# Cross-attention in a decoder kernel: scores turned by transposes, with the maximum subtracted on GpSimd

## The chip, the cores and the metric

The kernel runs on one core of a Trainium2 chip. The metric is the device time of one execution in microseconds; the lower the better.

## The reference

The program is a decoder of two layers over 8 sequences of 256 tokens of width 128: sliding-window attention with a memory that learns, a cross-attention, routed experts, causal attention, a gated recurrence, and a feed-forward mixture, each followed by a residual and a normalisation. The change lies in the cross-attention of the first layer and in the part of the memory's MLP that is computed in the same loop:

```python
# cross-attention: 16 heads of 8, query and context of 256 tokens
scores = einsum('bhqd,bhkd->bhqk', q, k) / sqrt(8)
scores = where(mask, scores, -1e9)
attn = softmax(scores, axis=-1)
x = einsum('bhqk,bhkd->bhqd', attn, v)
# memory MLP of the layer before it (updated weights)
out_mem = silu(x_in @ w1.T + b1) @ w2.T + b2
out_merged = sigmoid(out_swa @ lin1.T) * out_swa + sigmoid(out_mem @ lin2.T) * out_mem
```

The product of query and key is kept near f32 precision by splitting each into three bf16 parts; six pairs of parts are stacked along the contraction axis (6 x 16 = 96 rows).

## The kernel before, in words

Each engine has its own instruction stream, written by hand: PE (products and transposes), DVE, ACT, GpSimd (pool) and SyncE (sp), which issues the loads. They meet only through semaphores: an instruction adds to one (`then_inc`), and another engine waits for a count (`wait_ge`). The order inside an engine is the order of the code. PSUM has eight banks of 128 x 512 f32.

The cross-attention runs in four steps of NB = 2 batches (T = 512 tokens). Each engine has a function `mix(i, following)` for step i; three steps run in a loop (Fori) and the last stands behind it. A step has XU = 32 units, one for each pair of batch and head. Beside its own units, step i computes the *head* of step i+1: `keys` (the key projection) and parts 0 to 9 of `head`. Parts 0 to 3 are the four hidden chunks of the MLP (a product z, then Silu with the bias b1), part 4 the lin1 gate, part 5 the product with w2, part 6 the lin2 gate, parts 7 and 8 merge, normalise and transpose, and part 9 gives the query projection, which DVE splits into q_parts. The parts share bank 1. Tables (`early`, `later`) say behind which unit each part stands on each engine. The head of step 0 runs ahead of the loop, one part after another.

One unit, before:

- PE, `scores_q(n)` (L1074): two products give the scores with the queries on the partitions, 128 x 256 each, in one bank (`q_bank`). AHEAD = 14 units of them run ahead of the rest.
- DVE (L1815): a fused add of the mask and maximum over the keys, two per unit, written back to the bank; the maximum goes to `mx`. After every eight units PE transposes the maxima (`maxima_T`, L1084) and DVE negates them and splits them into three bf16 parts, `neg_max` (`negated`, L1804 to L1808).
- PE, `scores_k(n)` (L1102, L1104, L1105): the scores again, now with the keys on the partitions, plus the mask and the negated maximum as two further accumulating products; six products of 256 columns per unit. sT_ready.
- ACT (L1509): one exponential of 128 x 512 from the bank to `pT`.
- PE, `values(b, g)` (L1115): after four heads, eight products with `v_aug` (values and a column of ones, for the sum). ACT copies the result (`copy_outputs`, L1498), PE transposes it (`outputs_T`, L1127), DVE divides by the sum (L1831, L1834).

Behind a step's units comes the tail, the same in both kernels: output projection, residual, normalisation, router, ranks and slots of the experts (DVE, up to L1891). Then GpSimd scatters the tokens to the experts' rows with eight indirect DMAs (L817).

GpSimd otherwise splits the keys of the next step (`split_k`, L795 to L797), and makes add_q and add_k from the masks (L803, L804). SyncE saves the split parts to DRAM (`save_k`, `save_q`) and loads them back stacked (`stack`: 12 loads to `k_stack`, L658, and six to `q_stack`, L662). In a step the stack loads wait for sT_ready of all 32 units, since both kinds of scores read the stacks; the next step's first scores wait for them (L1064, L1065).

## Time and profile before

| | us |
|---|---|
| median of 3 runs | 1086.91 |
| lowest, highest | 1083.47, 1094.82 |
| the profiled execution, its device time | 1093.54 |
| its span, first to last instruction | 1091.5 |
| busy in the span: PE, DVE, ACT, GpSimd | 767.9, 529.8, 393.6, 158.9 |
| the four steps of this stage, from the first scores | from 342.6 to about 620 |
| mean granted clock of TensorE | 0.832 |

Durations below come from that one profiled execution. Its busy times are sums of an engine's instructions; matmuls are pipelined, so the spacing of their starts tells more than the length of one. The granted clock is given as a share of full speed: 1.0 is 2.4 GHz, 0.5 is 1.2 GHz. The releaser of a wait is inferred from the semaphores; "issue" is time in which an engine waited for nothing that the profile shows.

### The profile page before, as it was taken

To read this page: it belongs to the slowest core of one execution; us is meant where nothing else is said; L and a number is where in the kernel's file an instruction comes from. 1 tells how busy PE (TensorE), PEld (TensorE's weight loads), DVE (VectorE), ACT (ScalarE), POOL (GpSimd) and SP (SyncE) were. 2 spreads that over 40 slices of the span, in tenths; PEclk is the share of its full clock that TensorE was granted. 3 is DMA by queue.
4 is the path that set the end of the run, shared out by engine and by line. 5 is a ranking of instruction groups with operands and counts; after the bars stand their busy time and mean duration, and the time that the engine had idled before them with its cause. 6 is when DMAs were issued, how large, how long until landed. Compare 5 with 4: busy or idle time off the path is not lost.

```text
span 1091.5 us, 14695 instructions
## 1 busy us (share of the span) xinstructions
PE 767.9 (70%) x4586; PEld 496.2 (45%) x4586; DVE 529.8 (49%) x1947; ACT 393.6 (36%) x924; POOL 158.9 (15%) x207
## 2 busy tenths in 40 slices
PE   5888787968453986977968919992664664664664
PEld 4445353544121663653645617882442442442442
DVE  4244253443333945936939321112556556556556
ACT  3514434252111542533532513330343343343343
POOL 9200000000101004013012040002040040040020
PEclk8798998999566997997977959997887887887886
DMA  7400000000106035054040011311000010010000
GB/s 220 144 7 13 1 19 0 19 0 0 53 22 103 2 54 93 0 64 81 9 64 20 2 43 37 91 49 44 20 25 6 29 24 5 29 24 5 10 0 10
DMA packets 49236, 39.37 MB, mean 36 GB/s; under 512 B 11234, under 2 KB 42658, under 8 KB 49188
## 3 DMA queue, kind: packets, MB, share of 16 engines
q1 hardware_dynamic: 47140, 34.62, 14.7%
q0 software_dynamic: 2048, 4.20, 1.4%
q8 instruction: 19, 0.31, 0.1%
q14 instruction: 29, 0.24, 0.1%
HBM read 27.20 MB, written 11.60 MB: 36 GB/s over the span
## 4 chain that ended last, share of the span: by engine, by line
PE 52%; DVE 20%; issue 11%; ACT 8%; DMA 5%; POOL 2%; SPq 2%; DVEq 0%; POOLq 0%; ACTq 0%
PE bank L1219 4%; DMA q_stack<-parts_dram 4%; PE bank L1208 4%; DVE R L2066 2%; PE bank L1102 2%; PE bank L960 2%; PE bank L1105 2%; PE bank L1104 2%; PE bank L1115 2%; PE bank L892 2%; PE bank L1022 2%; PE bank L1074 2%; PE bank L1029 2%; PE bank L1298 2%; PE bank L983 2%
## 5 line engine op out<-in xcount | busy, mean ns | idle before, releaser
L1815 DVE CUSTOM_DVE_ANT_0 bank<-bank,add_q 128x256 f32<-128x256 f32 x256 | 100.2, 458 | 45.2 <-PE bank L1074 29.6
L1509 ACT ACTIVATE pT<-bank 128x512 f32<-128x512 f32 x128 | 76.1, 597 | 73.7 <-PE bank L1105 71.4
L1074 PE MATMUL bank<-k_stack,q_stack 96*128 96x256 bf16 x256 | 52.1, 303 | 40.0 <-DMA q_stack<-parts_dram 34.8
L1238 PE MATMUL bank<-ident,X 128*128 128x128 f32 x48 | 14.3, 420 | 89.7 <-DVE X L1923 89.7
L1102 PE MATMUL bank<-q_stack,k_stack 96*128 96x256 bf16 x256 | 70.4, 275 | 2.1 <-DVE mx L1815 2.1
L1104 PE MATMUL bank<-add_k,ident_b 128*128 128x256 bf16 x256 | 70.8, 276 | 0.0
L1105 PE MATMUL bank<-neg_max,head_sel 96*128 96x256 bf16 x256 | 70.7, 276 | 0.0
L1298 PE MATMUL bank<-XT,kpad 128*128 128x256 f32 (+1 forms) x256 | 59.1, 364 | 3.3 <-DVE cT L2023 3.2
L2023 DVE TENSOR_TENSOR cT<-bank,decay 128x384 f32<-128x384 f32 x64 | 35.7, 558 | 43.8 <-POOL decay L847 43.3
L1298 PEld LDWEIGHTS bank<-XT,kpad 128*128 128x128 f32 x256 | 47.9, 210 | 16.5 <-DVE cT L2023 9.5
L1074 PEld LDWEIGHTS bank<-k_stack,q_stack 96*128 96x128 bf16 x256 | 25.3, 105 | 64.8 <-DMA q_stack<-parts_dram 31.8
L1534 ACT ACTIVATE he<-bank 128x324 f32<-128x324 f32 x64 | 28.2, 441 | 69.4 <-PE bank L1208 63.9
L1238 PEld LDWEIGHTS bank<-ident,X 128*128 128x128 f32 x48 | 8.0, 167 | 98.7 <-DVE X L1923 95.5
L847 POOL TENSOR_SCALAR_AFFINE_SELECT decay<-decay 128x256 f32<-128x256 f32 x64 | 26.1, 408 | 142.8 <-ACT decay L1587 142.8
L795 POOL TENSOR_TENSOR qr<-g,k_parts 128x512 f32<-128x512 f32 x4 | 4.6, 1161 | 282.8 <-ACT k_parts L1480 282.7
L837 POOL DMA_INDIRECT pair_rows<-expert_out,spot_i x32 | 30.6, 956 | 102.9 <-DMA expert_out<-rows_y 93.2
L1219 PEld LDWEIGHTS bank<-moe_w,he 128*108 128x108 f32 x384 | 42.8, 173 | 1.3
L1219 PE MATMUL bank<-moe_w,he 128*108 128x128 f32 x384 | 43.1, 273 | 0.0
L1586 ACT ACTIVATE decay<-bank,a_col 128x256 f32<-128x256 f32 x64 | 30.6, 478 | 32.4 <-PE bank L1317 31.8
L1908 DVE COPY rows_y<-bank 108x384 f32<-108x384 f32 x16 | 8.9, 558 | 67.1 <-PE bank L1219 67.1
L1208 PE MATMUL bank<-rowsT,moe_w 128*128 128x324 f32 x128 | 39.1, 461 | 3.3 <-DVE rowsT L1900 3.3
L1404 ACT ACTIVATE probs<-probs,stats 128x192 f32<-128x192 f32 (+1 forms) x68 | 29.6, 436 | 20.5 <-DVE stats L1652 20.5
(401 smaller groups left out, 1775.0 us busy)
## 6 DMA issues: line engine op xcount, KB each, us to landing
k_stack<-parts_dram SPq DMA_DIRECT2D x48, 64.0 KB
q_stack<-parts_dram SPq DMA_DIRECT2D x24, 128.0 KB, 10.1
expert_in<-no_rows SPq DMA_DIRECT2D x8, 324.0 KB, 3.9
rows<-expert_in SPq DMA_DIRECT2D x8, 324.0 KB
expert_out<-rows_y SPq DMA_DIRECT2D x8, 324.0 KB
moe_w<-in_L_ffn_w_dram SPq DMA_DIRECT2D x1, 2048.0 KB
parts_dram<-k_parts SPq DMA_DIRECT2D x4, 384.0 KB, 2.7
parts_dram<-q_parts SPq DMA_DIRECT2D x12, 128.0 KB, 1.7
```

The source lines that it names most:

```text
L837: pool.indirect_dma_start(pair_rows[:, n, :], None, expert_out, bass.IndirectOffsetOnAxis(spot_i[:, n:n + 1], 0)).then_inc(gathered.sem, 16)
L1074: last = pe.matmul(q_bank(n)[:, c * S:(c + 1) * S], q_stack[:, h // 2, b * S + c * P:b * S + (c + 1) * P], k_stack[:, h // 2, h % 2, b * S ...
L1102: pe.matmul(dst, k_stack[:, h // 2, h % 2, b * S + c * P:b * S + (c + 1) * P], q_stack[:, h // 2, b * S:(b + 1) * S], start=True, stop=False)
L1104: pe.matmul(dst, ident_b[:], add_k[:, b * QC + c, :], start=False, stop=False)
L1105: last = pe.matmul(dst, head_sel[:, h % 8, :], neg_max[:, (n // 8) % 2, :], start=False, stop=True)
L1208: pe.matmul(bank[4 + n % 4][:, 0:HALF], moe_w1[:, e, k * P:(k + 1) * P], rowsT[:, e % 2, half * HALF:(half + 1) * HALF], start=True, stop= ...
L1219: last = pe.matmul(bank[2 + part][0:ROWS, t * P:(t + 1) * P], he[:, e % 2, k, col:col + ROWS], moe_w2[:, e, k, :], start=(k == 0), stop=(k ...
L1298: pe.matmul(m_banks(n)[1][:, lo:lo + width], kpad2[:, h, b * S + c * P:b * S + (c + 1) * P], XT[:, q0:q0 + width], start=True, stop=True)
L1509: act.activation(pT[:, g % 2, j], k_bank(n)[:].rearrange("p (c q) -> p c q", c=QC), ACT.Exp).then_inc(exp_ready.sem, 1)
L1586: act.activation(decay[:, n % DEEP, 0:S], eb[:, 0:S], ACT.Exp, bias=a_col[:, b * QC, h:h + 1])
L1815: last = dve.tensor_tensor_reduce(sc, sc, add_q[:, b * QC + c, :], 1.0, 2.0 * NEG, ALU.add, ALU.max, mx[:, c, h:h + 1])
L2023: dve.tensor_tensor(cT[:, g, j, :], m_banks(n)[1][:, 0:S + P], decay[:, n % DEEP, :], ALU.mult).then_inc(c_ready.sem, 1)
```

## The change

The second set of scores goes. DVE's fused add and maximum now writes the masked scores to SBUF, into one of SLIDE = 4 buffers `shifted`. GpSimd subtracts the row's maximum (stretched over 256 keys) in place for three units of four; for the fourth (`on_act`, n % 4 == 3) it only negates the maximum, and ACT takes the exponential in place with it as bias (two instructions of 128 x 256). PE then transposes the unit in four 128 x 128 blocks (`scores_T`) into one of two banks, and ACT's exponential takes it to `pT` (a plain copy in the fourth unit). The scores run LEAD = 3 units ahead instead of 14, since only three banks hold them, and DVE's unit n waits for the transposes of unit n - 4.

```diff
+                def scores_T(n):
+
+                    if on_act(n):
+                        pe.wait_ge(*p_ready.at(i, n // 4 + 1))
+                    else:
+                        pe.wait_ge(*s_shifted.at(i, n + 1))
+                    if n >= 2:
+                        pe.wait_ge(*exp_ready.at(i, n - 1))
                     for c in range(QC):
-                        dst = k_bank(n)[:, c * S:(c + 1) * S]
-                        pe.matmul(dst, k_stack[:, h // 2, h % 2, b * S + c * P:b * S + (c + 1) * P],
-                                  q_stack[:, h // 2, b * S:(b + 1) * S], start=True, stop=False)
-                        pe.matmul(dst, ident_b[:], add_k[:, b * QC + c, :], start=False, stop=False)
-                        last = pe.matmul(dst, head_sel[:, h % 8, :], neg_max[:, (n // 8) % 2, :], start=False, stop=True)
+                        for k in range(QC):
+                            last = pe.transpose(sT_bank(n)[:, k * S + c * P:k * S + (c + 1) * P], shifted[:, n % SLIDE, c, k * P:(k + 1) * P], ident[:])
                     last.then_inc(sT_ready.sem, 1)
...
+                for n in range(LEAD):
+                    scores(n)
+                for n in range(XU):
+                    if n + LEAD < XU:
+                        scores(n + LEAD)
+                    scores_T(n)
+                    if n >= 5 and n % 4 == 1:
+                        values((n // 4 - 1) // G, (n // 4 - 1) % G)
...
+                    if following and n == 1:
+                        keys(i + 1)
+                    if following and n in pe_at:
+                        head(i + 1, pe_at[n])
```

DVE and ACT, a unit:

```diff
                     wait_apart(dve, passed, *s_ready.at(i, n + 1))
+                    if n >= SLIDE:
+                        wait_apart(dve, passed, *sT_ready.at(i, n - SLIDE + 1))
                     for c in range(QC):
-                        sc = q_bank(n)[:, c * S:(c + 1) * S]
-                        last = dve.tensor_tensor_reduce(sc, sc, add_q[:, b * QC + c, :], 1.0,
-                                                        2.0 * NEG, ALU.add, ALU.max, mx[:, c, h:h + 1])
+                        last = dve.tensor_tensor_reduce(shifted[:, n % SLIDE, c, :], q_bank(n)[:, c * S:(c + 1) * S], add_q[:, b * QC + c, :], 1.0,
+                                                        2.0 * NEG, ALU.add, ALU.max, mx[:, n % SLIDE, c:c + 1])
                     last.then_inc(s_read.sem, 1)
...
+                    if on_act(n + 1):
+                        act.wait_ge(*s_shifted.at(i, n + 2))
+                        for c in range(QC):
+                            rows = shifted[:, (n + 1) % SLIDE, c, :]
+                            last = act.activation(rows, rows, ACT.Exp, bias=neg_mx[:, c:c + 1])
+                        last.then_inc(p_ready.sem, 1)
                     act.wait_ge(*sT_ready.at(i, n + 1))
...
-                    act.activation(pT[:, g % 2, j], k_bank(n)[:].rearrange("p (c q) -> p c q", c=QC), ACT.Exp).then_inc(exp_ready.sem, 1)
+                    act.activation(pT[:, g % 2, j], sT_bank(n)[:].rearrange("p (c q) -> p c q", c=QC), ACT.Copy if on_act(n) else ACT.Exp).then_inc(exp_ready.sem, 1)
```

GpSimd gets the units, and with them the scatters of the step before (one behind every third unit) and split_k (behind unit 4); add_k and its mask load go:

```diff
+            def heads(i, following):
+                for n in range(XU):
+                    wait_apart(pool, passed, *s_read.at(i, n + 1))
+                    if on_act(n):
+                        pool.tensor_scalar(neg_mx[:], mx[:, n % SLIDE], -1.0, None, ALU.mult).then_inc(s_shifted.sem, 1)
+                    else:
+                        pool.tensor_tensor(shifted[:, n % SLIDE], shifted[:, n % SLIDE], mx[:, n % SLIDE].unsqueeze(2).to_broadcast([P, QC, S]), ALU.subtract).then_inc(s_shifted.sem, 1)
+                    if following and n == 4:
+                        split_k(i + 1)
+                    if not is_first(i) and n % 3 == 2 and n // 3 < PAIRS:
+                        scatter(i - 1, n // 3)
                 if following:
+                    masks(i + 1)
```

Silu in the head's parts 0 to 3 becomes z (1 + tanh(z/2)), with the half taken at the w2 result: ACT computes the tanh and a copy of z with its bias, DVE the product. PE's next product into bank 1 waits for ACT's copy.

```diff
-                    act.activation(hT[:, n, 0:T], bank[1][:], ACT.Silu, bias=b1_new[:, n:n + 1]).then_inc(hT_b.sem, 1)
...
+                    act.activation(hT[:, n, 0:T], bank[1][:], ACT.Tanh, bias=b1_half[:, n:n + 1], scale=0.5)
+                    act.activation(z_of[n % 2], bank[1][:], ACT.Identity, bias=b1_new[:, n:n + 1]).then_inc(z_act.sem, 1)
...
+                    dve.scalar_tensor_tensor(hT[:, n, 0:T], hT[:, n, 0:T], 1.0, z_of[n % 2], ALU.add, ALU.mult).then_inc(hT_b.sem, 1)
```

The parts stand behind other units: on PE 0 to 9 behind units 3, 5, 7, 9, 11, 13, 15, 18, 23, 25, on ACT behind nearly the same, on DVE behind 7 to 28. The output transposes and divisions are done per half of the queries, those of batch 0 inside the step.

SyncE: the stack loads are split, and in a step they wait for the scores alone:

```diff
             save_k(0)
+            stack_k(0)
             save_q(0)
-            stack(0)
+            stack_q(0)
...
-                    sp.wait_ge(*sT_ready.at(i))
-                    stack(i + 1)
+                    sp.wait_ge(*s_ready.at(i))
+                    stack_k(i + 1)
+                    stack_q(i + 1)
```

How the streams now stand. PE, a unit deep in a step, before (the names are the stacked keys and queries, the mask, and the negated maxima):

```order
L1074 MATMUL bank4<-k_stack,q_stack 128x256 [waits s_read]
L1074 MATMUL bank4<-k_stack,q_stack 128x256
L1102 MATMUL bank6<-q_stack,k_stack 128x256 [waits exp_ready]
L1104 MATMUL bank6<-add_k,ident_b 128x256
L1105 MATMUL bank6<-neg_max,head_sel 128x256
```

The last three rows stand twice per unit, once for each half of the keys. PE after the change, unit 3 with the head's part 0 behind it and the next unit (k_copied is the semaphore under p_ready):

```order
L1103 MATMUL bank<-k_stack,q_stack 128x256 [waits s_read]
L1103 MATMUL bank<-k_stack,q_stack 128x256
L1111 ISA
L1118 MATMUL bank<-ident,shifted 128x128 [waits exp_ready,k_copied]
L1118 MATMUL bank<-ident,shifted 128x128 x3
L1050 ISA
L1051 REGISTER_ALU [waits b_x_loaded]
L1054 MATMUL bank<-xT_in,w1T_new 128x512 [waits kf_ready]
```

The unit's transposes now wait for ACT (in the other three of four for GpSimd's s_shifted), and the head's product stands right behind them. GpSimd in the loop, before:

```order
L795 TENSOR_TENSOR qr<-g,k_parts 128x512 [waits kh_ready]
L84 ISA
L796 CAST k_parts<-qr 128x512 [waits pool_b]
L101 REGISTER_ALU
L797 TENSOR_TENSOR k_parts<-qr,k_parts 128x512 [waits pool_b]
L84 ISA
L84 ISA [waits sT_ready]
L803 TENSOR_SCALAR add_q<-mask_q 128x1024 [waits masks_loaded]
L804 TENSOR_SCALAR add_k<-mask_k 128x1024
```

GpSimd in the loop after the change, units 2 to 5 (max_a is the semaphore under slots_ready, L831 the subtraction, L829 the negation):

```order
L831 TENSOR_TENSOR shifted<-shifted,mx 128x512 [waits s_read]
L84 REGISTER_ALU
L823 DMA expert_in<-Xm,slot_i 6208x128 [waits max_a]
L84 REGISTER_ALU
L829 TENSOR_SCALAR neg_mx<-mx 128x2 [waits s_read]
L84 REGISTER_ALU
L831 TENSOR_TENSOR shifted<-shifted,mx 128x512 [waits s_read]
L807 REGISTER_ALU
L809 TENSOR_TENSOR qr<-g,k_parts 128x512 [waits kh_ready]
L84 ISA
L810 CAST k_parts<-qr 128x512 [waits pool_b]
```

The scatters, which stood in one block behind the tail, and split_k now stand between the units' subtractions.

## Rows read from the trace of the kernel before

**Rows 1.** windows: a step's scores, then what lies between two steps; busy us (x instructions)

```profile
342.60:398.30 55.70, 52.28 (x413) 33.97 (x416) 41.16 (x174) 30.37 (x49) 3.16 (x4) 0.97 0.07 22
398.30:419.00 20.70, 8.69 (x79) 6.70 (x72) 9.17 (x55) 3.04 (x10) 5.62 (x6) 0.72 1.00 110
419.00:475.60 56.60, 53.57 (x416) 33.95 (x420) 40.60 (x174) 30.40 (x49) 9.79 (x11) 0.95 0.09 30
```

**Rows 2.** page, part 5; busy us, mean ns of one, idle before and its releaser

```profile
L1815 DVE CUSTOM_DVE_ANT_0 bank<-bank,add_q 128x256 f32<-128x256 f32 x256 | 100.2, 458 | 45.2 <-PE bank L1074 29.6
L1509 ACT ACTIVATE pT<-bank 128x512 f32<-128x512 f32 x128 | 76.1, 597 | 73.7 <-PE bank L1105 71.4
```

**Rows 3.** timeline of PE in step 0; start us, us

```profile
350.45 1.13 PE L1022 MATMUL bank<-xT_in,w1T_new 128*128 128x512 f32 x2 [0.34 <-ACT hT L1458]
...
356.22 3.70 PE L1029 MATMUL bank<-hT,w2T_new 128*128 128x512 f32 x8 [0.30 <-ACT g L1462]
...
360.86 0.27 PE L1102 MATMUL bank<-q_stack,k_stack 96*128 96x256 bf16 x1
360.97 0.27 PE L1104 MATMUL bank<-add_k,ident_b 128*128 128x256 bf16 x1
...
371.20 0.60 PE L1037 MATMUL bank<-ident,g 128*128 128x128 f32 x4
...
379.73 1.07 PE L1115 MATMUL bank<-pT,v_aug 128*32 128x256 f32 x16
```

**Rows 4.** timeline around the steps' ends; engine (SPq: SyncE's queue), line, idle before

```profile
324.80 4.18 SPq L658 DMA_DIRECT2D k_stack<-parts_dram  x12
...
342.64 0.60 PE L1074 MATMUL bank<-k_stack,q_stack 96*128 96x256 bf16 x2 [19.97 <-DMA q_stack<-parts_dram]
...
395.74 2.59 ACT L1509 ACTIVATE pT<-bank 128x512 f32<-128x512 f32 x4
...
397.81 4.12 SPq L658 DMA_DIRECT2D k_stack<-parts_dram  x12
...
416.88 0.17 DVE L1891 TENSOR_TENSOR gates_all<-share,found 128x8 f32 x1
...
418.97 0.61 PE L1074 MATMUL bank<-k_stack,q_stack 96*128 96x256 bf16 x2 [5.15 <-DMA q_stack<-parts_dram]
...
424.44 0.43 DVE L1815 CUSTOM_DVE_ANT_0 bank<-bank,add_q 128x256 f32<-128x256 f32 x1 [7.39 <-issue]
...
572.73 0.43 DVE L1815 CUSTOM_DVE_ANT_0 bank<-bank,add_q 128x256 f32<-128x256 f32 x1 [0.85 <-PE bank L1074]
...
617.74 2.59 ACT L1509 ACTIVATE pT<-bank 128x512 f32<-128x512 f32 x4 [0.15 <-PE bank L1105]
```

**Rows 5.** groups of GpSimd, shapes kept apart; columns as in rows 2

```profile
L817 POOL DMA_INDIRECT expert_in<-Xm,slot_i x32 | 31.4, 980 | 34.2 <-DVE slot_i L1886 25.7 <-issue 8.5
...
L843 POOL TENSOR_SCALAR v_aug<-ctx_tok 128x512 f32<-128x512 f32 x4 | 6.0, 1498 | 90.8 <-DVE X L1923 90.8
L789 POOL TENSOR_TENSOR x_res<-memT,x_bo_rows 128x512 f32<-128x512 f32 x4 | 5.1, 1264 | 23.5 <-DVE memT L1772 23.5
L795 POOL TENSOR_TENSOR qr<-g,k_parts 128x512 f32<-128x512 f32 x4 | 4.6, 1161 | 282.8 <-ACT k_parts L1480 282.7
```

**Rows 6.** timeline of GpSimd

```profile
346.57 1.15 POOL L795 TENSOR_TENSOR qr<-g,k_parts 128x512 f32<-128x512 f32 x1 [27.27 <-ACT k_parts L1480]
...
418.71 0.98 POOL L817 DMA_INDIRECT expert_in<-Xm,slot_i  x1 [0.30 <-issue]
...
655.12 0.15 POOL L831 MEMSET v_aug<- 128x32 f32 x1
```

**Rows 7.** timeline of ACT in step 0

```profile
346.51 1.28 ACT L1458 ACT_TABLE_LOAD   x1
347.81 0.69 ACT L1458 ACTIVATE hT<-bank,b_new 128x512 f32<-128x512 f32 x1
```

**Rows 8.** window early in the last step; PE, PEld, DVE, ACT, POOL, PEclk, DMA, GB/s

```profile
574.00:584.00 10.00, 6.17 (x25) 2.31 (x24) 9.86 (x48) 0.00 (x0) 6.03 (x7) 0.50 0.12 46
```

More of the change, by code:

```diff
@@ L822, in _ @@
             pool.wait_ge(*slots_zero.at(0))
-            with pool.Fori(0, STEPS - 1) as i:
-                mix(i, True)
-            mix(STEPS - 1, False)
+            heads(0, True)
+            with pool.Fori(0, STEPS - 2) as i:
+                tail(i, True)
+                heads(i + 1, True)
+            tail(STEPS - 2, True)
+            heads(STEPS - 1, False)
+            tail(STEPS - 1, False)
+            for n in range(PAIRS):
+                scatter(STEPS - 1, n)
             pool.wait_ge(*scattered.at(STEPS - 1))
@@ L1057, in values_of @@
                 last.then_inc(v_b.sem, 1)
-            early = {0: "keys", 2: 0, 4: 1, 6: 2, 8: 3, 10: 4, 12: 5}
-            later = {4: 6, 9: 7, 17: 8, 20: 9}
             def mix(i, following):
@@ L1110, in values @@
                     pe.wait_ge(*exp_ready.at(i, b * H1 + 4 * g + 4))
+                    if b == 0 and g == 0:
+                        pe.wait_ge(*slots_ready.before(i))
                     if g % 2 == 0 and (b > 0 or g > 0):
@@ L1125, in outputs_T @@
                     for g in range(G):
-                        for c in range(QC):
-                            last = pe.transpose(bank[2 + c][:, g * P:(g + 1) * P], o_heads[:, g, c * P:(c + 1) * P], ident[:])
+                        last = pe.transpose(o_bank(b, c)[:, g * P:(g + 1) * P], o_heads[:, g, c * P:(c + 1) * P], ident[:])
                     last.then_inc(o_tr.sem, 1)
-                for n in range(AHEAD):
-                    scores_q(n)
-                    if n == 9:
-                        maxima_T(0)
-                    if following and n in early:
-                        if n == 0:
-                            keys(i + 1)
-                        else:
-                            head(i + 1, early[n])
@@ L1837, in mix @@
+                    if following and n in dve_at:
+                        head(i + 1, dve_at[n], head_chain)
+                for c in range(QC):
+                    outputs_of(1, c)
                 if following:
@@ L2074, in _ @@
             head_chain = Chain(dve, dve_h, 0)
-            for n in range(4, 10):
+            for n in range(10):
                 head(0, n, head_chain)
```

193 lines of the change are left out of this document (80 added, 113 removed).

## The prediction, made before the changed kernel had run

> **What bounds the kernel now.** I read the cores' spans first (one core, 1091.5 us), then the windows. The change touches the cross-attention stage: a prologue, four steps of 32 head units, and a serial tail behind each step. In the windows [rows 1] a step's scores run 55.7 us in step 0 and 56.6 us in step 1; PE is busy 52.3 and 53.6 us of them, at a granted clock of 0.97 and 0.95 of 2.4 GHz. DVE has 41, ACT 30, GpSimd 3 to 10 us. So PE bounds this stretch. The groups of the page say the same: ACT's exponential idled 73.7 us, nearly all until PE's L1105, and DVE's masked maximum until PE's L1074 [rows 2]. The timeline gives PE's price by start to start at full clock: a 256-column bf16 product every 0.11 us [rows 3], so a unit costs PE 2 + 6 of them, 0.88 us.
>
> Between two steps lie 20.7 us [rows 1] in which PE works 8.7 us, the clock falls and the 16 DMA engines are busy throughout. The timeline [rows 4] shows why: the last exponential of step 0 ends at 398.3, the stack loads go out from 397.81 (they wait for sT_ready of all units), PE's next scores start at 418.97, released by the q_stack load, and DVE's first maximum only at 424.44, after 7.39 us marked issue, which is neither data nor a semaphore; DVE's tail had ended at 417.05. Behind step 2 there is no such gap (the loop is left there): DVE starts at 572.73.
>
> **The change, part by part.** PE: six products per unit (0.66 us) become four 128x128 f32 transposes. Four took 0.60 us [rows 3] with about 0.27 of pipeline end in it, so 0.11 each and 0.44 a unit. Over 32 units that is 7 us off; the eight small transposes of the maxima go too. What is left on PE in a step: units 32 x 0.66 = 21.1; eight value products at 1.0 = 8.0; the first half's output transposes 0.9; of the next step's head seven products at 0.97 = 6.8, w2 3.5, two sets of transposes 0.9, q 0.9 [rows 3]. Sum 42.1 us, against 52.3 busy before.
>
> DVE: the same two reductions per unit, 100.2 us / 128 = 0.78 us a unit [rows 2], now written to SBUF instead of PSUM; I take the same price (bounds: 0.1 us less or more). The negated maxima go, four products come, priced at 0.69 us each, which is what ACT's Silu of that shape takes [rows 7]. DVE stays near 37 us.
>
> GpSimd is new in the chain. The trace has no 128x512 subtraction with a stretched operand in two rows of 256; the bounds are 1.16 us (two plain operands) and 1.50 us (one operand, 16-column pieces), and nearest is 1.26 us, a two-operand add with a repeated operand [rows 5]. I take 1.27 with its start. The negated maximum of the fourth unit has 256 numbers: 0.15 us for a tiny memset [rows 6] up to 0.35; I take 0.25. A step then costs 24 x 1.27 + 8 x 0.25 = 32.5 us, plus split_k's three instructions 3.1, plus, from step 1 on, eight scatters of the step before at 0.98 + 0.30 = 1.28 [rows 5, 6] = 10.2. Sum: 35.6 in step 0, 45.8 in steps 1 and 2, 42.7 in step 3. GpSimd, idle so far, becomes the longest engine in three steps of four.
>
> Whether it slows beside DVE: with the maxima running, L795 took 1.15 us against a group mean of 1.16 [rows 6, 5]; no cost. The Trainium skill's SBUF page ("Who interferes with whom") says that a VectorE instruction with two SBUF inputs shuts out a GpSimd instruction that reads SBUF. The maximum has one of its inputs in PSUM, so by the rule it stays free and the trace agrees. By the same rule the new products of the head, both operands in SBUF, would each hold back one subtraction by up to 0.7 us, some 3 us a step. I leave that out of the sum.
>
> ACT: 32 exponentials or copies at 0.60 = 19.2 [rows 2]; 16 exponentials of half the size, at most 0.5 each = 8; four output copies 2.4; keys 1.3; four times Tanh and Identity at 0.69 = 5.5; 2.3 for the rest; a table load fewer (1.28 [rows 7]; Tanh and Exp share a set, Silu did not), two left = 2.6. Some 41 us. In units 3 to 10 it needs 3.0 us for two units, so it paces those, at 1.5 to 1.7 us a unit; GpSimd's scatters (1.4 us a unit there) lie beside it.
>
> Time of a step. Step 0: PE's 42.1, the pipe to fill before the first transposes (0.8 + 1.3) and to drain (0.6), and 3 us since PE starts at 1.2 GHz: 48 against 55.7, so -7.7. Steps 1 and 2, from DVE's start: GpSimd's 45.8, fill and drain 2.2, and 3 us for stalls around the 3.5 us w2 block, over which only three units lie ready: 51, against 475.6 - 424.44 = 51.2 in step 1 (step 2 is alike): 0 each. Step 3: 42.7 + 2.2 + 2 cold = 47 against 620.3 - 572.7 = 47.6: -0.6.
>
> Between steps. SyncE now waits for s_ready of all units, which PE reaches at n=28, about 3 units before the end; q's saves hang on DVE's head part 9, at the same place. So the loads start some 3 us earlier, and so does all that is behind them in the DMA queues. PE's scores could start 3 us earlier; DVE's start after the 7.39 us gap I take 3 us earlier too, since the gap ends just after the DMA traffic does (bounds 0 and 5). Behind step 2 DVE's own tail ends 0.85 us before it starts; at most 0.5 is won. Together -6.5. The scatters no longer stand between the tail and split_k; nothing waits for either there.
>
> Prologue. The head of step 0 runs one part after another, PE waiting for ACT to free the bank; Identity adds 4 x 0.69 = +2.8 us. But the 12 key loads no longer wait behind q: from the first stack load, 324.80, to the scores, 342.64, were 17.8 us [rows 4], and the six q loads are half the bytes: 8.9 us. With the saves before them I take -8 (bounds 0 and -10). Net -5.
>
> Sum: -5 - 7.7 - 0 - 0 - 0.6 - 6.5 = -19.8 us. The profiled execution took 1093.54 us, so 1073.7 for it. It lies 6.6 above the median of the three runs, 1086.91, and from that the sum gives 1067.
>
> **The rivals.**
> A, GpSimd's subtraction is dearer and nothing is won. At the upper bound of 1.50 us (L843 [rows 5]) 96 of them cost 96 x 0.23 = 22 us more, in three steps fully on the path, with held-back starts by DVE in it: 1067 + 22 = 1089. For it: GpSimd's rows for one shape differ by 0.35 us, and each instruction now has a wait. Against: L843's odd pieces.
>
> B, slower: PE stays at 1.2 GHz. Early in step 3 PE was busy 62% for ten microseconds and the clock stayed at 0.5 [rows 8]; only a solid block of products raised it. The Trainium skill's TensorE page ("PE-mode transpose") says the full clock does not engage for transposes. With the clock at half a unit costs PE 0.44 + 0.88 + 0.5 for its share of the values = 1.8 us. In step 3, which has no head, all 32 units would run so: 58 + 3 = 61 instead of 47, +14. In the others the clock would rise with w2 (unit 13); until then 13 x 1.32, six products at 2.1 and two value blocks at 2 make 34 us instead of 21: +13, three times. 1067 + 53 = 1120. It decides once PE is slower than GpSimd, at 1.27 us a unit. Against: each step's head products start early, and before they raised the clock within 4 to 6 us; step 3 has value blocks every fourth unit. Nothing in the trace is a long run of transposes, so it can't be excluded.
>
> C, the engines overlap without the stalls that I added and the loads land earlier: steps of 45, 48, 48, 45 and 2 us more in each gap: 1067 - 11 - 6 = 1050, or less if a subtraction costs 1.16 (-8): 1042.
>
> **How the numbers follow.** Forecast 0.50 (own range 1053 to 1078), A 0.23, B 0.13, C 0.14. The range 1040 to 1104 takes in C and A and leaves out B's far end. A measurement of this kernel can tell about 1% (11 us) from no change. Faster by more: C and nine tenths of the forecast, 0.59. Slower: B and a few hundredths of A beyond its bound, 0.16. Within 1%: the rest, 0.25.
>
> **What would show it.** Right: GpSimd near 46 us busy in steps 1 and 2 and the longest engine, its subtraction at 1.2 to 1.3 us start to start, transposes 0.11 us apart with the clock near 1, first scores of step 0 near 335, DVE's first maximum of step 1 some 23 us after the last exponential. Wrong: transposes 0.21 us apart deep in a step (B); subtractions at 1.5 us or waits of PE on s_shifted in all units (A); steps over 55 us with no engine full, which would mean that the ring DVE, GpSimd, PE, ACT with four buffers is bound by its handovers, and none of my sums.

## The result, and the profile after

The changed kernel is slightly slower: 1093.26 us median (1086.06 to 1098.77, 20 runs) against 1088.76 (1081.56 to 1094.82, 20 runs), ratio 1.004 with a 95% interval of 1.0021 to 1.0059. The forecast was 1067. The profiled execution's span is 1097.0 us against 1091.5; these two executions took 1098.77 and 1093.54 us, both some 5 above their kernel's median, and the steps below are read from them.

The page's busy times and costliest groups after (columns as in [rows 2]):

```profile
PE 753.1 (69%) x4298; PEld 485.6 (44%) x4298; DVE 517.8 (47%) x1884; ACT 422.0 (38%) x1001; POOL 268.6 (24%) x330
...
L1834 DVE CUSTOM_DVE_ANT_0 shifted<-bank,add_q 128x256 f32<-128x256 f32 x256 | 95.2, 420 | 76.7 <-PE bank L1103 67.8
L831 POOL TENSOR_TENSOR shifted<-shifted,mx 128x512 f32<-128x512 f32 x96 | 100.4, 1060 | 91.2 <-DVE mx L1834 75.0
L1525 ACT ACTIVATE pT<-bank 128x512 f32<-128x512 f32 x128 | 75.4, 596 | 95.9 <-PE bank L1118 94.5
L1118 PE MATMUL bank<-ident,shifted 128*128 128x128 f32 x512 | 86.7, 297 | 34.3 <-POOL shifted L831 20.7
```

PE is busy 15 us less, GpSimd 110 us more, and the time is no better. The last columns tell how that can be: DVE waits for PE's scores, GpSimd for DVE's maxima, PE for GpSimd, ACT for PE. Each engine waits for the one ahead of it, and the four form a ring; before, DVE and ACT waited mostly for PE [rows 2]. GpSimd's subtraction, feared at up to 1.50 us, takes 1.06.

The windows after, cut as [rows 1], with step 3 as a fourth: step 0, the gap, step 1, step 3.

```profile
329.69:390.42 60.73, 49.80 (x344) 30.99 (x344) 36.68 (x158) 37.09 (x68) 32.33 (x36) 0.90 0.13 32
390.42:406.39 15.97, 8.31 (x71) 6.53 (x71) 7.36 (x43) 3.01 (x9) 2.26 (x2) 0.78 1.06 106
406.39:474.20 67.81, 51.20 (x344) 31.59 (x344) 40.72 (x172) 37.19 (x68) 41.00 (x44) 0.85 0.12 31
577.74:622.49 44.75, 35.88 (x318) 24.59 (x314) 27.43 (x150) 26.60 (x51) 34.34 (x40) 0.89 0.04 13
```

In step 1 no engine is full: PE 51 of 67.8 us, GpSimd and DVE 41. PE is still the busiest, and its busy time has hardly fallen: 51.2 us against 53.6 in step 1, 49.8 against 52.3 in step 0 [rows 1]. Below, a step is measured from DVE's first maximum to the last exponential, and a gap from there to DVE's next first maximum:

| us | step 0 | step 1 | step 2 | step 3 | three gaps |
|---|---|---|---|---|---|
| before | 54.9 | 51.1 | 51.0 | 47.6 | 26.1, 26.6, 19.6 |
| after | 59.9 | 62.3 | 61.1 | 41.2 | 21.5, 24.6, 21.5 |
| after less before | +5.0 | +11.2 | +10.1 | -6.4 | -4.6, -2.0, +1.9 |

So +19.9 in the steps and -4.7 in the gaps. The prologue, from its first load (xT_in, 279.93 before, 275.57 after) to the first scores, went from 62.7 to 54.1 us, -8.6. The stage itself began 4.4 us earlier, ahead of all changed code; in the executions profiled here that start lies between 269.5 and 283.7, so profiled executions are compared by step and not by total. What lies behind the last exponential is 3.4 us longer, in unchanged code. The five add up to the difference of the spans, +5.6 us.

How far two executions of the same code differ is seen where an edit left the steps alone. The run with the old order of the loads (below) has the steps of the changed kernel and took 59.9, 60.0, 61.5 and 41.3 us; the same reading of the two versions of the kernel before (below) gives a gap that differs by 3.4 us. So a difference under some 2 us in one step, or 3.5 us in one gap, shows nothing by itself. Step 1 in the changed kernel and in that run:

```profile
411.95:474.20 62.25, 49.74 (x338) 30.86 (x338) 38.72 (x158) 37.19 (x68) 41.00 (x44) 0.88 0.11 29
420.06:480.08 60.02, 47.16 (x338) 29.48 (x338) 38.98 (x158) 37.04 (x68) 40.99 (x44) 0.94 0.11 28
```

The longer one has the lower granted clock. In it the clock was at 1.2 GHz not only at the start but once more in the middle of the step, behind waits of 0.37 and 1.40 us of PE for GpSimd, and PE worked through this stretch:

```profile
454.13:457.53 3.40, 3.40 (x25) 1.69 (x24) 1.40 (x8) 2.84 (x6) 2.61 (x4) 0.50 0.06 22
```

The place where a step with a head loses is seen in three stretches of step 1. PE at its start, and in the MLP's region (start us, us):

```profile
406.39 1.46 PE L1103 MATMUL bank<-k_stack,q_stack 96*128 96x256 bf16 x6 [0.76 <-DMA q_stack<-parts_dram]
412.79 0.61 PE L1103 MATMUL bank<-k_stack,q_stack 96*128 96x256 bf16 x2 [4.94 <-DVE mx L1834]
414.01 1.11 PE L1118 MATMUL bank<-ident,shifted 128*128 128x128 f32 x4 [0.61 <-POOL shifted L831]
...
416.19 1.91 PE L1084 MATMUL bank<-ctxT,w_L_xattn_wkT 128*128 128x512 f32 x2
...
428.65 0.65 PE L1118 MATMUL bank<-ident,shifted 128*128 128x128 f32 x4 [1.27 <-ACT shifted L1520]
429.14 1.02 PE L1054 MATMUL bank<-xT_in,w1T_new 128*128 128x512 f32 x2
430.00 0.38 PE L1103 MATMUL bank<-k_stack,q_stack 96*128 96x256 bf16 x2
430.23 0.60 PE L1118 MATMUL bank<-ident,shifted 128*128 128x128 f32 x4
```

GpSimd, DVE and ACT around the w2 block, which keeps PE busy from 439.7 to 443.3:

```profile
440.26 1.04 POOL L831 TENSOR_TENSOR shifted<-shifted,mx 128x512 f32<-128x512 f32 x1 [0.80 <-DVE mx L1834]
444.92 1.04 POOL L831 TENSOR_TENSOR shifted<-shifted,mx 128x512 f32<-128x512 f32 x1 [3.62 <-DVE mx L1834]
```

```profile
443.96 0.42 DVE L1834 CUSTOM_DVE_ANT_0 shifted<-bank,add_q 128x256 f32<-128x256 f32 x1 [3.88 <-PE bank L1103]
```

And the other way round, DVE in the head's part 9 (two of its five instructions left out) and PE behind it:

```profile
464.75 0.75 DVE L1800 TENSOR_SCALAR g<-bank,x_bq 128x512 f32<-128x512 f32 x1 [0.78 <-PE bank L1079]
...
466.72 0.43 DVE L1804 CAST q_parts<-qr 128x512 bf16<-128x512 f32 x1
467.18 0.69 DVE L1806 TENSOR_TENSOR q_parts<-qr,q_parts 128x512 bf16<-128x512 f32 x1
467.79 0.42 DVE L1834 CUSTOM_DVE_ANT_0 shifted<-bank,add_q 128x256 f32<-128x256 f32 x1
```

```profile
466.15 0.63 PE L1118 MATMUL bank<-ident,shifted 128*128 128x128 f32 x4
469.84 0.66 PE L1118 MATMUL bank<-ident,shifted 128*128 128x128 f32 x4 [3.06 <-POOL shifted L831]
```

A block of 3.5 us on PE stops DVE for 3.88 and GpSimd for 3.62; a block of 3.0 us on DVE stops PE for 3.06. Nothing is in hand on either side. And at the step's start PE stands idle 4.94 us for DVE's first maximum. DVE came as late before (424.44, 5.47 us behind PE's first scores; 411.95, 5.56 us behind, after), and what held it there the profile does not show, but PE then ran the head's keys and part 0 meanwhile:

```profile
419.50 2.08 PE L1051 MATMUL bank<-ctxT,w_L_xattn_wkT 128*128 128x512 f32 x2
...
422.35 2.08 PE L1022 MATMUL bank<-xT_in,w1T_new 128*128 128x512 f32 x2
```

### The profile page after: what moved, and what is told of

The parts are those of the page before. It is cut to its first block, busy times and chain, and to the rows that moved or that the text cites. A ratio compares the mean times of both kernels' runs of the same rounds, so it can differ in the third digit from the quotient of the medians.

```text
span 1097.0 us, 14728 instructions
## 1 busy us (share of the span) xinstructions
PE 753.1 (69%) x4298; PEld 485.6 (44%) x4298; DVE 517.8 (47%) x1884; ACT 422.0 (38%) x1001; POOL 268.6 (24%) x330
## 4 chain that ended last, share of the span: by engine, by line
PE 49%; DVE 21%; issue 13%; ACT 9%; POOL 5%; DMA 2%; DVEq 1%; SPq 0%; POOLq 0%; ACTq 0%
PE bank L1229 4%; PE bank L1218 4%; PE bank L1118 3%; PE bank L1130 3%; DVE R L2073 2%; PE bank L992 2%; PE bank L924 2%; PE bank L1308 2%; POOL shifted L831 2%; PE bank L1015 2%; DVE shifted L1834 2%; PE bank L980 2%; PE bank L1062 1%; PE bank L1017 1%; PE bank L1054 1%
## 5 line engine op out<-in xcount | busy, mean ns | idle before, releaser
L1834 DVE CUSTOM_DVE_ANT_0 shifted<-bank,add_q 128x256 f32<-128x256 f32 x256 | 95.2, 420 | 76.7 <-PE bank L1103 67.8
L831 POOL TENSOR_TENSOR shifted<-shifted,mx 128x512 f32<-128x512 f32 x96 | 100.4, 1060 | 91.2 <-DVE mx L1834 75.0
L1118 PE MATMUL bank<-ident,shifted 128*128 128x128 f32 x512 | 86.7, 297 | 34.3 <-POOL shifted L831 20.7
L1118 PEld LDWEIGHTS bank<-ident,shifted 128*128 128x128 f32 x512 | 63.5, 151 | 51.5 <-POOL shifted L831 28.8
L1103 PE MATMUL bank<-k_stack,q_stack 96*128 96x256 bf16 x256 | 54.1, 303 | 24.7 <-DVE mx L1834 13.7
L1308 PE MATMUL bank<-XT,kpad 128*128 128x256 f32 (+1 forms) x256 | 62.2, 378 | 3.2 <-DVE cT L2030 3.2
L1308 PEld LDWEIGHTS bank<-XT,kpad 128*128 128x128 f32 x256 | 50.2, 219 | 17.2 <-DVE cT L2030 8.8
L1103 PEld LDWEIGHTS bank<-k_stack,q_stack 96*128 96x128 bf16 x256 | 26.1, 107 | 50.0 <-DVE mx L1834 19.0
L1503 ACT ACTIVATE log_var<-mv,eps 128x2 f32<-128x2 f32 x34 | 9.8, 289 | 80.3 <-DVE mv L1770 80.0
```

The costliest lines, as they stand in the source:

```text
L831: pool.tensor_tensor(shifted[:, n % SLIDE], shifted[:, n % SLIDE], mx[:, n % SLIDE].unsqueeze(2).to_broadcast([P, QC, S]), ALU.subtract).t ...
L1103: last = pe.matmul(q_bank(n)[:, c * S:(c + 1) * S], q_stack[:, h // 2, b * S + c * P:b * S + (c + 1) * P], k_stack[:, h // 2, h % 2, b * S ...
L1118: last = pe.transpose(sT_bank(n)[:, k * S + c * P:k * S + (c + 1) * P], shifted[:, n % SLIDE, c, k * P:(k + 1) * P], ident[:])
L1308: pe.matmul(m_banks(n)[1][:, lo:lo + width], kpad2[:, h, b * S + c * P:b * S + (c + 1) * P], XT[:, q0:q0 + width], start=True, stop=True)
L1834: last = dve.tensor_tensor_reduce(shifted[:, n % SLIDE, c, :], q_bank(n)[:, c * S:(c + 1) * S], add_q[:, b * QC + c, :], 1.0, 2.0 * NEG, A ...
```

## The experiments

Where no range of times is given, a version ran once. Steps and gaps are each from one profiled execution, with the spread told above.

**A deeper ring.** Scores 5 units ahead instead of 3, six buffers `shifted` instead of four, two of `neg_mx`, and DVE's head parts two units later.

```diff
-        LEAD = 3
-        SLIDE = 4
+        LEAD = 5
+        SLIDE = 6
```

> The changed kernel with a deeper pipe: scores run 5 units ahead instead of 3, six buffers of masked scores instead of four, two negated maxima, and DVE's parts of the head two units later. In the changed kernel the steps run 59.9, 62.3, 61.1 and 41.2 us from DVE's first maximum to the last exponential. Theory R (ring: with three units of lead every head part that blocks one engine stops all of them, once its length exceeds what lies ready): the three steps with a head lose 4 to 9 us each, the last at most 1; total -12 to -25 us. Theory G (GpSimd's work, with scatters and port waits, sets the step): no step moves by more than 1 us.

Measured: 1083.62 us median (1081.03 to 1087.95, 10 runs) against 1087.23, ratio 0.9974 (0.9941 to 1.0007). Steps 56.5, 56.2, 56.4, 40.5: 3.4, 6.1 and 4.7 us less than after. The window of step 1 from DVE's first maximum, and who PE waits for in it (us in total, times, longest), the same view of after behind it:

```profile
408.20:464.40 56.20, 45.99 (x338) 28.91 (x338) 44.31 (x158) 36.53 (x68) 39.85 (x44) 0.95 0.09 27
```

```profile
PE bank L1118 <- ACT shifted L1520: 5.8, 5, 1.4
PE bank L1103 <- DVE mx L1834: 4.3, 1, 4.3
PE bank L1118 <- POOL shifted L831: 1.0, 1, 1.0
```

```profile
PE bank L1118 <- POOL shifted L831: 6.5, 5, 3.1
PE bank L1103 <- DVE mx L1834: 4.9, 1, 4.9
PE bank L1118 <- ACT shifted L1520: 3.1, 3, 1.3
```

The waits for GpSimd fall from 6.5 to 1.0 us; those for ACT's in-place exponential grow from 3.1 to 5.8. The version wins back about half of the loss in steps 1 and 2 (6.1 of 11.2 and 4.7 of 10.1 us), and the next handover of the ring takes over. Part of it may be the clock, 0.95 in step 1 against 0.88; the two were not separated. The three gaps are 3.0 us longer in all, and the device time, each version against the kernel before as it ran beside it, falls by 0.7% and not by the 14.8 us of the four steps.

**Part 9 in pieces.** DVE's five instructions for the query parts spread over the last four units.

```diff
-25: 8, 28: 9}
+25: 8, 28: 13, 29: 10, 30: 11, 31: 12}
```

> The changed kernel, but the five DVE instructions of head part 9 (3.0 us in a row behind unit 28) are spread behind units 28 to 31. Theory R: GpSimd's idle time of 3.5 us and PE's of 3.1 us near the end of the steps with a head go, each such step is 2 to 3 us shorter. Theory G: nothing moves. In both the query parts are saved up to 3 us later, so the gap behind the step can grow by that.

Steps 57.2, 58.7, 58.8, 41.2, that is 2.7, 3.6 and 2.3 us less than after, where PE had waited 3.06 us. PE's longest wait for GpSimd in step 1 is 1.4 us now, but its waits there add up to 15.2 us against 15.8, and the clock is 0.95 against 0.88:

```profile
417.45:476.16 58.71, 46.19 (x338) 28.90 (x338) 38.95 (x158) 37.07 (x68) 41.93 (x44) 0.95 0.07 23
```

So removing the block helped, and the higher clock has a part in it that was not separated. The gaps grew by 3.3, 1.8 and -0.4, perhaps since q's parts are saved later, so the total, 1098.5, shows nothing.

**The scatters in one block.** GpSimd's eight scatters again behind the tail, as before the change.

```diff
-                    if not is_first(i) and n % 3 == 2 and n // 3 < PAIRS:
-                        scatter(i - 1, n // 3)
...
+                for n in range(PAIRS):
+                    scatter(i, n)
```

> The changed kernel, but the eight scatters stand in one block behind the tail, as before the change, not between the units. Theory G: steps 1 and 2 lose most of the 8 x 1.2 = 10 us of scatters and come to the length of step 0 or under, 52 to 60 us, and step 3 loses the same, to 32 to 36 us. Theory R: steps 1 and 2 lose 0 to 3 us, step 3 (41.2 us, no head) loses 4 to 10 us since only there GpSimd is the longest engine. The block may delay the start of steps 1 to 3 by some us, as GpSimd's first subtraction stands behind it.

1116.91 us, steps 58.3, 65.1, 66.3, 47.5. GpSimd in front of step 1's first subtraction:

```profile
416.84 1.21 POOL L823 DMA_INDIRECT expert_in<-Xm,slot_i  x1 [6.40 <-DVE slot_i L1891]
...
426.01 0.97 POOL L823 DMA_INDIRECT expert_in<-Xm,slot_i  x1 [0.30 <-issue]
427.00 3.04 POOL L831 TENSOR_TENSOR shifted<-shifted,mx 128x512 f32<-128x512 f32 x3
```

DVE's first maximum was at 420.78, and the first subtraction stands 6.2 us behind it. This is worse, so the scatters between the units are well placed. Counted from GpSimd's first subtraction step 1 took 58.8 us against 61.3: without the scatters between the units it is 2.5 us shorter, not 10, so they are not the main part of what makes the steps long.

**No unit with the bias on ACT.** GpSimd subtracts in all 32 units.

```diff
-            return n % 4 == 3
+            return False
```

> The changed kernel, but GpSimd subtracts in all 32 units and ACT never takes an exponential in place. GpSimd gets 8 x (1.06 - 0.37) = 5.5 us a step more, ACT 8 us less. Theory G: every step 3 to 6 us longer, the last one too. Theory R with ACT's order as the cause (ACT takes the exponential of unit 3, 7, 11 behind a head part, PE waited 1.27 us for it): steps with a head 2 to 5 us shorter, the last step longer by 3 to 6 us.

1100.25 us, steps 58.2, 62.6, 60.4, 44.7. In the steps with a head the eight subtractions more on GpSimd cost nothing that can be told (-1.7, +0.3, -0.7); in step 3, which has none, they cost 3.5. So GpSimd's work sets the pace where there is no head, and does not where there is one.

**ACT's parts one unit later.** They stand behind the next exponential, so that unit 7's and 11's in-place exponentials come ahead of them.

```diff
-        act_at = {3: 0, 5: 1, 7: 2, 9: 3, 11: 4, 15: 6,
+        act_at = {4: 0, 6: 1, 8: 2, 10: 3, 12: 4, 15: 6,
```

> The changed kernel, but ACT takes the head's parts 0 to 4 one unit later (behind units 4, 6, 8, 10, 12), so that it does not stand and wait for PE's product. In the changed kernel two units take 3.65 us in this region, in which PE, ACT and GpSimd all idle. Theory V (convoy: product on PE, then Tanh and Identity, then the exponentials, each in order behind the other; a loop of two engines): the period falls to about 3.0 us and steps 0 to 2 lose 3 to 4 us each, step 3 nothing. Theory G (GpSimd's work sets the step): no change.

1094.93 us, steps 60.1, 61.9, 60.5, 41.2, all within 0.6 of after. PE's waits for L1520 in step 1 fall from 3.1 to 2.2 us, and 3.0 us of new waits for ACT stand ahead of the head's products: what is taken from one wait comes back in another.

**w2 in four pieces.** PE's block of eight products behind units 12 to 15, two at a time; the parts 5 and 6 stand one unit later on ACT and DVE too.

```diff
-                if n == 5:
+                if n == 5 or n >= 50:
...
-        pe_at = {... 11: 4, 13: 5, 15: 6, ...}
+        pe_at = {... 11: 4, 12: 50, 13: 51, 14: 52, 15: 53, 16: 6, ...}
```

> The changed kernel, but the 3.5 us block of w2 products on PE is taken in four pieces behind units 12 to 15, and the parts 5 and 6 stand one unit later. Theory R (a block on one engine stops the ring): the 3.6 us in which DVE and GpSimd idle behind unit 13 go, steps 0 to 2 lose 2 to 3 us each, the last nothing. Theory G: no change.

1092.96 us, steps 60.8, 63.6, 63.8, 41.2: 0.9, 1.3 and 2.7 longer, where 2 to 3 shorter was expected; only the last is clear of the spread. DVE's longest wait for PE in step 1 fell from 3.9 to 2.2 us, so the edit did what it should, while PE's own waits came to 17.9 us for 15.8. While PE runs w2 it works, and the others' idle time then is not lost for PE's sum.

**All together.** The deeper ring, w2 in pieces, ACT's parts later, part 9 behind the last unit, keys behind the first scores.

```diff
+                    if following and n == 2:
+                        keys(i + 1)
...
+        pe_at = {3: 0, 5: 1, 7: 2, 9: 3, 11: 4, 13: 50, 14: 51, 15: 52, 16: 53, 18: 6, 20: 7, 24: 8, 26: 9}
+        act_at = {4: 0, 6: 1, 8: 2, 10: 3, 12: 4, 19: 6, 22: 7, 25: 8}
+        dve_at = {10: 0, 12: 1, 14: 2, 16: 3, 18: 4, 22: 5, 24: 6, 26: 7, 28: 8, 31: 9}
```

> The changed kernel with everything together: 5 units of lead and six buffers, ACT's parts one unit behind PE's, w2 in four pieces, head part 9 on DVE behind the last unit, key projection before the units (in the gap in which PE waits for DVE). If theories R and V name the whole loss, steps 0 to 2 come near the busy time of their longest engine, GpSimd's 42 to 44 us and PE's 42, and take 48 to 52 us instead of 59.9, 62.3 and 61.1; total 1058 to 1070. If the port shared by DVE and GpSimd or GpSimd's work holds them, they stay at 55 to 57 us, as with the deeper pipe alone, total about 1082.

1088.37 us (1085.62 to 1096.79, 10 runs), ratio 0.9994 (0.9957 to 1.0031); steps 56.1, 57.8, 57.1, 40.6. No better than depth alone: the gains of single edits do not add.

**The head out of the steps.** Deeper ring; keys, split_k and all ten parts behind the units.

```diff
-                    if following and n in pe_at:
-                        head(i + 1, pe_at[n])
...
+                    keys(i + 1)
                     values_of(i + 1)
+                    for n in range(10):
+                        head(i + 1, n)
```

> The deeper version (scores 5 units ahead, 6 buffers, 2 of the negated maxima) with keys, split_k and all ten parts of the next step's head taken out from between the units and put behind them, on every engine. It tells how much of a step is units alone. Read from DVE's first maximum to the last exponential, steps 0 to 2 were 56.5, 56.2, 56.4 us in the deeper version and step 3, which has no head, 40.5. Theory H (the units' ring is fast by itself, 40 to 42 us, whatever else PE, DVE and ACT do; the head's parts between the units cost their own 16 us): steps 0 to 2 fall to 40 to 43 us, with the scatters still among them. Theory S (something in the looped steps other than the head holds them, the cold clock at their start, the scatters or the late start of DVE): they stay above 48. The whole kernel gets slower under both, since the head then runs one part after another: the gaps between the steps grow by 20 to 27 us each, device time 1105 to 1125.

1159.87 us. Steps 35.8, 40.7, 40.6, 40.6; gaps 64.3, 67.0, 61.6, so 40 us more each and not 20 to 27. The windows of steps 0 and 1:

```profile
335.33:371.12 35.79, 33.65 (x310) 24.01 (x307) 24.20 (x132) 25.99 (x51) 27.10 (x33) 0.92 0.04 10
435.41:476.10 40.69, 35.25 (x306) 24.55 (x306) 24.61 (x132) 26.50 (x51) 35.36 (x41) 0.90 0.04 14
```

This is the run that divides a step. The units alone take 35.8 us; with the eight scatters, and behind a late start of DVE, 40.7 (+4.9, GpSimd then being the fullest beside PE). The head adds 20.7 us in step 0 and 15.5 in step 1 of the deeper version. PE's work for the head comes to 12.1 us at full clock by the prediction's own prices (6.8 + 3.5 + 0.9 + 0.9): in this ring the head comes on top of the units, with 3 to 9 us more. The windows say how: PE is busy 33.65 of the 35.8 us in the units alone, so there is little room on it. Of the 15.5 us in step 1 of the deeper version 10.7 are more busy time of PE (45.99 against 35.25) and 4.8 more idle time. Before the change a head added 3.5 us in steps 1 and 2 (51.1 less 47.6) and 7.3 in step 0. The 3.5 flatter the kernel before: keys and part 0 stood ahead of DVE's first maximum there, and step 3 ran at a clock of 0.83. Counted from the first scores a head added 7.3 to 8.2 us before and 16 to 23 after the change.

**The head's products left out.** Deeper ring; DVE's four products z (1 + tanh) give way to a tiny instruction, so the MLP's hidden values are wrong.

```diff
-                    dve.scalar_tensor_tensor(hT[:, n, 0:T], hT[:, n, 0:T], 1.0, z_of[n % 2], ALU.add, ALU.mult)
+                    dve.tensor_scalar(hT[:, n, 0:2], hT[:, n, 0:2], 1.0, None, ALU.add)
```

> The deeper version with the head's four products of 128x512 on DVE (z times one plus tanh, both operands in SBUF) left out: DVE adds 1 to two columns instead, so the MLP's hidden values are tanh(z/2) and not silu. Theory L (the product keeps GpSimd's subtraction out and is itself kept waiting by it, 0.7 to 3.5 us instead of 0.69): steps 0 to 2 fall by 2 to 4 us each, from 56.5, 56.2, 56.4 to some 53, device time down by 6 to 12. Theory N (DVE has slack there, the stalls sit elsewhere in the head): under 1 us a step, device time within 3 us.

1086.37 us, steps 56.5, 55.9, 56.7, 40.5: within 0.3 of the deeper version. The products were held up badly (last section), 22.6 us for twelve instead of 8.3, and taking them away gives nothing, though DVE is busy 40.9 us in step 1 instead of 44.3. So DVE's busy time is not the bound either. PE's waits of 1.26 us for ACT's L1520 stand as they did.

**Keys and parts 0 and 1 back in the gap.** Deeper ring; on PE they stand behind the first three scores, on ACT ahead of the units, and DVE's parts 0 and 1 behind units 4 and 6.

```diff
+                    if following and n == 2:
+                        keys(i + 1)
+                        head(i + 1, 0)
+                        head(i + 1, 1)
```

> The deeper version with keys and the head's parts 0 and 1 moved from behind units 1, 3 and 5 to the start of the step, behind the first three scores, as they stood before the change: PE and ACT wait there for DVE's first maximum anyway (PE idled 4.9 us in step 1 of the changed kernel). Theory F (part of the lost time is that the old order filled this gap with the head and the new one does not): each step with a head gets 2 to 4 us shorter from first scores to last exponential, the TensorE clock rises earlier, device time down by 6 to 10 from the deeper version's 1083.6 to some 1075, ratio to before 0.988. Theory N: moving them gains nothing, within 2 us of 1083.6.

1082.71 us (1079.13 to 1087.08, 10 runs), ratio 0.9976 (0.9944 to 1.0007). Steps 60.0, 55.7, 55.1, 40.6, gaps 23.2, 23.7, 18.9. From the first scores to the last exponential step 1 took 61.0 us, as in the deeper version (464.36 - 403.28 = 61.1), and step 0 took 3.5 more: in step 0 there is no idle gap to fill (DVE starts 0.8 us behind the scores), so 6 us of head work delayed the units. Nothing of the 6 to 10 us expected.

**The loads' order alone.** The kernel before, with only the 12 key stack loads of the prologue ahead of q's saves.

```diff
             save_k(0)
+            stack_k(0)
             save_q(0)
-            stack(0)
+            stack_q(0)
```

> The kernel before, with one part of the change alone: in the prologue of the stage the 12 key loads go out before the query parts are saved, not behind them. The prologue (first load of the stage to the first scores, 62.7 us before, 54.1 in the changed kernel, which also has 2.3 us more of Identity) should shorten by 10 to 11 us, the steps stay: total 1077 to 1080. If the loads only ran faster in the changed kernel for another reason (one mask load less), it stays within 2 us.

1075.53 us (1071.98 to 1077.37, 4 runs) against 1089.79, ratio 0.9862 (0.9819 to 0.9904). PE's wait ahead of the first scores is 9.47 us in place of 19.97 [rows 4], and the prologue 52.1 us in place of 62.7:

```profile
327.69 0.61 PE L1078 MATMUL bank<-k_stack,q_stack 96*128 96x256 bf16 x2 [9.47 <-DMA q_stack<-parts_dram]
```

This version is faster than both kernels: one piece of the change, made alone.

**The changed kernel with the old order of those loads.**

```diff
-            stack_k(0)
             save_q(0)
+            stack_k(0)
             stack_q(0)
```

> The changed kernel with only the order of the loads in the prologue put back: the 12 key stack loads go out behind the saves of q's parts again, as before the change. It closes the account of the change. The same edit made alone on the kernel before gave 1075.5 against 1089.8 us, 10.6 of them in the prologue. Theory P (the change holds one gain, the loads' order, and without it the turned scores cost the steps' +20 less the gaps' -5): the prologue from the first load to the first scores goes from 54.1 to 62 to 66 us, device time 1101 to 1107, ratio to before 1.012 to 1.018. Theory Q (in the changed kernel the prologue waits for something else, the Identity copies or GpSimd's share, and the loads' order matters little): the prologue stays under 58 us, device time within 4 us of 1093.

1107.69 us (1099.66 to 1110.33, 4 runs) against 1088.37, ratio 1.0201 (1.015 to 1.0251): 14 us above the changed kernel's median. Prologue 68.1 us (269.49 to 337.61), more than the 62 to 66 expected:

```profile
337.61 1.46 PE L1103 MATMUL bank<-k_stack,q_stack 96*128 96x256 bf16 x6 [24.01 <-DMA q_stack<-parts_dram]
```

So the account closes from both sides. Without the loads' order the change costs 2.0% (some 19 us); the loads give back 14.

## Why the prediction was wrong, point by point

- **Gaps and prologue: right in sign and nearly in size.** Gaps -6.5 predicted, -4.7 found; the nearness is partly luck. By gap it was -3, -3, -0.5 against -4.6, -2.0, +1.9, and in four executions that share these gaps they sum to 61.6 to 67.6 us, in two before to 69.3 and 72.3. Prologue -5 predicted, -8.6 found: the loads gave 10.6 (alone) instead of 8, Identity cost 2.3 instead of 2.8.
- **The instructions' prices: right or too high.** Subtraction 1.06 us for 1.27, so rival A falls as a mechanism, though the time came out near its 1089. DVE's maximum into SBUF 0.42 us for 0.46. GpSimd in step 1 was busy 41.0 us for 45.8, ACT 37.2 for 41. The negation is 0.37 for 0.25. But ACT and its handovers do not let two units pass in the 3.0 us counted in the MLP's region: value products, one block for four units, start at 424.38 and 431.70, so 3.66 us.
- **Rival B falls.** Windows of after: the start of step 1, the units behind it, and step 3, which has no head, early and late:

```profile
406.40:419.00 12.60, 7.05 (x26) 4.44 (x27) 5.77 (x35) 2.02 (x4) 5.49 (x6) 0.50 0.10 30
419.00:440.00 21.00, 16.82 (x127) 9.90 (x126) 14.38 (x53) 17.04 (x32) 17.71 (x18) 0.98 0.10 32
581.00:589.00 8.00, 5.83 (x31) 4.58 (x32) 5.29 (x29) 3.07 (x6) 6.35 (x8) 0.61 0.03 8
589.00:622.00 33.00, 28.61 (x278) 19.29 (x275) 19.60 (x104) 23.05 (x46) 27.99 (x33) 1.00 0.05 16
```

  In step 3 PE runs transposes, scores and values only, and stays at 2.4 GHz for 33 us. By the rule that full clock does not engage for transposes (the Trainium skill, "TensorE: Matmul & The Clock Gate", "PE-mode transpose") step 3 would have taken 61 us, by the estimate of the prediction; it took 41.2. The trace does not agree with the rule for such a mix; whether transposes alone would raise the clock no run here shows.
- **Time of a step: the term that failed.** For steps 0 to 2 I wrote 48, 51 and 51; they took 59.9, 62.3, 61.1. The step of the working is "fill and drain 2.2, and 3 us for stalls around the 3.5 us w2 block, over which only three units lie ready": I took the fullest engine's busy time and added a few stalls. The runs show that this holds only where a step has nothing but units: 41.2 in step 3 (47 predicted; the fall of 6.4 was put at 0.6), and 35.8 in step 0 with its head taken out. With a head, its parts on PE stop the ring's other engines and its parts on DVE and ACT stop PE, and the head comes on top: 15.5 to 20.7 us in the deeper version, some 20 in the changed one. PE waits 15.8 us in step 1 of after, by the three rows quoted under the deeper ring and two of 0.7 and 0.6 us for DVE. From DVE's first maximum PE, the fullest engine, is idle 12.5 of 62.3 us; before it was 3.0 of 51.1. The working allowed 5.2 us for fill, drain and stalls. The listed condition, "steps over 55 us with no engine full", is what came.
- **A second term, PE's own load at its clock.** The prediction made GpSimd the longest engine, with 45.8 us, and gave PE 42.1 us at full clock, with 3 us for the cold start in step 0 and none in steps 1 and 2. GpSimd was busy 41.0 us in step 1, PE 49.7. In after PE idles 4.94 us at the start of step 1 and works at 1.2 GHz until 419, 7 us at double price; the clock is down again in the middle of the step (454.13 to 457.53). Before, the head's keys and first products ran there and DVE's start found the clock at 1.00. The window from DVE's first maximum in step 1 of before:

```profile
424.44:475.53 51.09, 48.06 (x406) 31.91 (x404) 40.60 (x174) 27.81 (x46) 5.49 (x7) 1.00 0.06 20
```

  So PE's load fell by 2.4 us from the first scores (53.6 to 51.2), not by the 10 counted. That moving the head back there gains nothing in the deeper ring was a surprise to me; in step 0 the parts delay the units instead.
- **w2 as the culprit: wrong place.** I had put the stall at the w2 block; cutting it up made no step shorter.

What stays open: which handover holds the deeper version at 56 us, how much of the stalls acts through the clock that falls behind them, and what holds DVE's first maximum. PE waits 5.8 us in it for ACT's in-place exponentials, but in the shallower ring moving the head's parts away from them, or giving those units to GpSimd, moved the wait and did not remove it. An ordering that would remove it was not found.

## What to carry to other kernels

Fullest engine plus fill and drain came near the step's time here only in the steps without other work among the units. Before, PE had up to 14 units of scores out ahead of its second scores; the change made a ring of four engines with three units in hand, and the head interleaved in it was paid in full and more. Five units in hand took 6 us off step 1 and left the rest. So count units in hand against the foreign blocks on each engine, beside busy time, and price the fullest engine's work at the clock that its own waits will leave it. And try each piece of a large change alone: here a moved block of twelve loads, alone, gave 1.4%, and the change that held it gave nothing.

## What the runs showed of the hardware that I had not expected

DVE and GpSimd hold each other up. In step 1 of after DVE's product with both operands in SBUF:

```profile
424.25 2.35 DVE L1777 SCALAR_TENSOR_TENSOR hT<-hT,g 128x512 f32<-128x512 f32 x1 [1.09 <-ACT g L1473]
...
427.90 1.16 DVE L1777 SCALAR_TENSOR_TENSOR hT<-hT,memT 128x512 f32<-128x512 f32 x1
...
435.16 0.69 DVE L1777 SCALAR_TENSOR_TENSOR hT<-hT,memT 128x512 f32<-128x512 f32 x1
```

```profile
423.90 1.06 POOL L823 DMA_INDIRECT expert_in<-Xm,slot_i  x1 [0.16 <-issue]
424.99 1.05 POOL L831 TENSOR_TENSOR shifted<-shifted,mx 128x512 f32<-128x512 f32 x1
426.00 0.69 POOL L829 TENSOR_SCALAR neg_mx<-mx 128x2 f32<-128x2 f32 x1
427.48 1.04 POOL L831 TENSOR_TENSOR shifted<-shifted,mx 128x512 f32<-128x512 f32 x1 [0.79 <-DVE mx L1834]
```

The product takes 0.69 us with GpSimd idle. At 427.90 it met a subtraction in flight, which ended at 428.5, and its own end came 0.54 behind that. At 424.25 it began beside a scatter, outlasted that and the subtraction behind it, and ended at 426.60, and then the negation of two columns, begun at 426.00, took 0.69 in place of 0.21 to 0.25. In the deeper version the twelve products average 1.88 us. The prediction put the price on GpSimd, "up to 0.7 us" a product; most of it fell on DVE. The Trainium skill ("SBUF — State Buffer", "Who interferes with whom") says that a VectorE instruction with two SBUF inputs contends with a GpSimd instruction that reads SBUF, and that the order of issue decides who blocks. The trace agrees with the first: the maxima, with one operand in PSUM, show no such growth (0.41 to 0.43 us beside GpSimd or without). With the second it agrees at 427.90, where the subtraction was first; at 424.25 the product had begun 0.74 us ahead of the subtraction, and that still took its usual 1.05 us. What it cost in time cannot be told from nothing: the run without the products has the same steps within 0.3 us.

The order of the loads gave more than the 8.9 us counted by bytes. In the kernel before with that order alone the key loads went out 15.3 us behind the first load, in place of 44.9, and the scores came 10.6 us earlier. Putting them back made the changed kernel's prologue 14.0 us longer, 3.4 more than the same edit gave before, with PE's wait at 24.01 us against 19.97. Why the same queue order waits 4 us longer there stays open. In device time the two edits are alike, some 14 us between the medians, so 4 us of the gain before lie outside the prologue, and nothing here says where.
